# The last product of a feed-forward layer, taken from rounded parts and turned back by two transposes

## What is computed

```python
def _tlin(x, w, s):
    return jnp.einsum('bsi,oi->bso', x, w) * s      # w holds -1, 0 and 1
h = jax.nn.silu(_tlin(x, w1_w, w1_s)) * _tlin(x, w2_w, w2_s)   # 128 -> 512
h = jax.nn.gelu(_tlin(h, h1_w, h1_s), approximate=False)       # 512 -> 512
h = jax.nn.gelu(_tlin(h, h2_w, h2_s), approximate=False)       # 512 -> 512
return _tlin(h, w3_w, w3_s)                                    # 512 -> 128
```

## Time and profile before

| what | value |
|---|---|
| median of 3 runs | 1271.09 us (1270.57 to 1271.78) |
| profiled execution | 1273.35 us, of which the span from first to last instruction is 1271.5 us |
| TensorE clock granted, mean of the span | 0.976 |
| PE busy | 1152.8 us, 91% |
| VectorE busy | 986.7 us, 78% |
| ScalarE busy | 771.9 us, 61% |
| GpSimd busy | 568.4 us, 45% |
| feed-forward layer | about 1071 us to the end, 200 us |

### The profile page before, as it was taken

How to read it: one execution, slowest core, us unless ns; L and a number is a source line. 1 busy time by engine, 2 the same in 40 slices (tenths; PEclk the granted TensorE clock), 3 DMA queues, 4 the chain that set the end, 5 groups by cost and what they waited for, 6 DMA issues and landing times.

```text
span 1271.5 us, 32080 instructions
## 1 busy us (share of the span) xinstructions
PE 1152.8 (91%) x10554; PEld 941.7 (74%) x10554; DVE 986.7 (78%) x2499; ACT 771.9 (61%) x2314; POOL 568.4 (45%) x729
## 2 busy tenths in 40 slices
PE   3888886789898869999999999999999997999997
PEld 3555554688888747777777777777777766999997
DVE  6688885588888777778788778787877876788885
ACT  2445553222222249888989888899888894344342
POOL 2777775444444554444545445445444342011112
PEclk9999998799999989999999999999999998999999
DMA  8000000000000000000000000000000000000000
GB/s 282 10 2 0 0 1 2 1 2 1 0 1 0 1 1 2 1 2 1 2 2 1 0 0 0 0 0 0 0 0 0 2 1 1 6 13 12 8 12 19
DMA packets 14303, 12.32 MB, mean 10 GB/s; under 512 B 1778, under 2 KB 12564, under 8 KB 13972
## 3 DMA queue, kind: packets, MB, share of 16 engines
q1 hardware_dynamic: 14228, 11.34, 2.9%
HBM read 9.24 MB, written 2.10 MB: 9 GB/s over the span
## 4 chain that ended last, share of the span: by engine, by line
PE 56%; DVE 14%; issue 8%; POOL 4%; ACT 1%; DVEq 1%; POOLq 0%; ACTq 0%
PE bank L191 14%; PE bank L976 10%; PE bank L1041 10%; PE bank L1070 10%; PE bank L1083 5%; PE bank L840 4%; POOL rstd L365 2%; DVE stat L298 2%; DVE hT L1230 1%; DVE gg L1222 1%; PE bank L795 1%; DVE yn L314 1%; POOL X L370 1%; DVE mv L303 1%; DVE fh_hi L1191 1%
## 5 line engine op out<-in xcount | busy, mean ns | idle before, releaser
L993 ACT ACTIVATE work<-bank,work 128x256 f32<-128x256 f32 x512 | 236.0, 474 | 60.0 <-DVE work L985 59.2
L985 DVE TENSOR_REDUCE work<-bank 128x2 f32<-128x512 f32 x256 | 164.0, 682 | 113.2 <-PE bank L976 113.2
L1007 POOL TENSOR_TENSOR work<-work 128x512 f32<-128x512 f32 x64 | 66.7, 1041 | 279.0 <-DVE work L1001 279.0
L959 POOL TENSOR_TENSOR work<-work 128x512 f32<-128x512 f32 x128 | 164.3, 1284 | 30.2 <-DVE work L951 15.8
L1013 ACT ACTIVATE work<-work 128x256 f32<-128x256 f32 x384 | 161.7, 509 | 0.0
L1041 PE MATMUL bank<-ident,work 128*128 128x128 f32 x1024 | 141.9, 279 | 5.1 <-DVE work L949 1.6
L1041 PEld LDWEIGHTS bank<-ident,work 128*128 128x128 f32 x1024 | 111.7, 141 | 38.5 <-issue 19.9
L1070 PE MATMUL bank<-work 128*64 128x256 f32 x1024 | 138.5, 392 | 0.5 <-DVE work L1056 0.5
L840 PE MATMUL bank<-WrT,moe_work 128*128 128x128 f32 x1024 | 137.4, 278 | 0.7 <-POOL moe_work L817 0.7
L363 POOL TENSOR_SCALAR ve<-mv 128x2 f32<-128x2 f32 x128 | 28.6, 223 | 240.1 <-DVE mv L303 240.1
L976 PE MATMUL bank<-work 32*128 32x256 f32 x2048 | 130.4, 391 | 2.6 <-ACT work L993 1.6
(11 more groups left out here) (176 smaller groups left out, 2903.9 us busy)
## 6 DMA issues: line engine op xcount, KB each, us to landing
X<-in_x SPq DMA_DIRECT2D x4, 512.0 KB, 5.9
wF<-in_L_ffn_h_w SPq DMA_DIRECT2D x2, 1024.0 KB, 9.7
out<-X SPq DMA_DIRECT2D x16, 128.0 KB, 1.8
w_qkv<-in_L_attn_w_qkv SPq DMA_DIRECT2D x1, 1536.0 KB, 9.2
WrT<-in_L_ffn_Wr SPq DMA_DIRECT2D x1, 1024.0 KB, 5.1
w_out<-in_L_attn_w_out SPq DMA_DIRECT2D x1, 512.0 KB, 10.5
wF<-in_L_ffn_w_w SPq DMA_DIRECT2D x2, 256.0 KB, 8.5
rope_sin<-in_rope_sin SPq DMA_DIRECT2D x1, 256.0 KB, 3.2
```

The lines of the kernel that those rows point to most:

```text
L959: nc.gpsimd.tensor_tensor((QT if kind == "q" else KT)[:, p, a, :], rc[:, ru % 2, :], rs_[:, ru % 2, :], ALU.add).then_inc(c_rope, 1)
L985: nc.vector.tensor_reduce(nmax[:, QUAD * a + j, :], SB_[j][:, :].rearrange("p (t k) -> p t k", t=T), AX.X, ALU.max, negate=True).then_inc( ...
L993: ins = nc.scalar.activation(pr[:, a % 2, j, t, :], SB_[j][:, t * LEN:(t + 1) * LEN], ACT.Exp, bias=nmax[:, h, t:t + 1], accum_out=psum_[: ...
```

## The change

The last product takes parts as the others do. ScalarE rounds `f2` into `f2_hi` (one copy of 128 x 512 behind each half of the gelu), and GpSimd forms `f2_lo = f2 - f2_hi` in two halves at the head of its next step, in front of `rstd` and the residual add. The weight w3 moves into `wF`, so that the test covers it (`wF` grows from 5120 to 5632 columns, `CHECK` from 320 to 352), and gets its parts `w3_hi` (GpSimd, step 0) and `w3_lo` (VectorE, step 0). The product is turned: w3 is stationary, `f2` moves in blocks of 256 tokens, and the result lies by features in `bank7`. ScalarE copies it to `yT`, and two transposes on TensorE bring it back into `Yt`; they stand between the two halves of the second hidden product, which is issued in halves for that. The last sequence keeps the old product behind its last gelu.

```diff
-        wF = sb("wF", [P, (2 + 2 * HID_T) * HID_T * P])
+        wF = sb("wF", [P, (2 + 2 * HID_T) * HID_T * P + HID_T * E])
-        w3T = sb("w3T", [P, HID_T, E])
+        w3T = wF[:, (2 + 2 * HID_T) * HID_T * P:].rearrange("p (k e) -> p k e", k=HID_T)
...
+        ffn_weights.append((w3T, w3S[0][:, :, :], w3S[1][:, :, :]))
+        W3_PIECE = len(ffn_weights) - 1
...
-        def ffn_product(pe, src, wS, written, emptied, base, short):
-            for m in range(2):
+        def ffn_product(pe, src, wS, written, emptied, base, short, halves=range(2)):
+            for m in halves:
...
+        def ffn_round_scalar(act, i, m):
+            b = slice(2 * m, 2 * m + 2)
+            act.wait_ge(d_a2, 2 * i + m + 1)
+            act.wait_ge(d_yt, reached(i))
+            nc.scalar.activation(f2S[0][:, b, :], f2[:, b, :], ACT.Copy).then_inc(d_f2hi, 1)
+
+        def ffn_rest_pool(pool, i):
+            for m in range(2):
+                b = slice(2 * m, 2 * m + 2)
+                wait_apart(pool, d_f2hi, 2 * i + m + 1, s_nhalf, 1)
+                nc.gpsimd.tensor_tensor(f2S[1][:, b, :], f2[:, b, :], f2S[0][:, b, :], ALU.subtract).then_inc(d_f2s, 1)
+
+        def ffn_out_turned_tensor(pe, i, short):
+            if i_is(i, 0):
+                pe.wait_ge(n_xnT[3], SEQS)
+                pe.wait_ge(d_w, EARLY + HID_T + 1)
+            pe.wait_ge(d_f2s, 2 * (i + 1))
+            pe.wait_ge(d_yc, reached(i))
+            for kb in range(HID_T):
+                ins = split_product(VB[:, 0:LEN], (w3S[0][:, kb, :], w3S[1][:, kb, :]),
+                                    (f2S[0][:, kb, :], f2S[1][:, kb, :]), kb == 0, kb == HID_T - 1, short)
+            ins.then_inc(d_yt, 1)
+
+        def ffn_out_scalar(act, i):
+            act.wait_ge(d_yt, i + 1)
+            act.wait_ge(d_y, reached(i))
+            nc.scalar.activation(yT[:, :], VB[:, 0:LEN], ACT.Copy).then_inc(d_yc, 1)
+
+        def ffn_back_tensor(pe, i):
+            pe.wait_ge(d_yc, i + 1)
+            pe.wait_ge(y_ready[FFN], reached(i))
+            for t in range(T):
+                ins = nc.tensor.transpose(Yt[:, t, :], yT[:, t * P:(t + 1) * P], ident[:, :])
+            ins.then_inc(d_y, 1)
...
 # GpSimd, ffn_step(i, p)
-                if not (i_is(i, 0)):
+                if i_is(i, 0):
+                    pool.wait_ge(c_v, 2 * QUADS * SEQS)
+                    ffn_weights_pool(pool, (W3_PIECE,))
+                else:
+                    ffn_rest_pool(pool, i - 1)
                     norm_pool(pool, 4, i - 1, 0)
...
 # VectorE, ffn_step(i, p), behind ffn_in_vector(dve, i + 1)
+                if i_is(i, 0):
+                    ffn_weights_vector(dve, (W3_PIECE,))
...
 # ScalarE, ffn_step(i, p)
-                act.wait_ge(d_y, reached(i))
-                gelu(i, 1, f2, d_m2, d_a2)
+                if not i_is(i, 0):
+                    ffn_out_scalar(act, i - 1)
+                    act.wait_ge(d_f2s, 2 * i)
+                for m in range(2):
+                    gelu(i, 1, f2, d_m2, d_a2, (m,))
+                    if not i_is(i, SEQS - 1):
+                        ffn_round_scalar(act, i, m)
...
 # TensorE, ffn_step(i, p)
-                        ffn_out_tensor(pe, i - 1)
+                        ffn_out_turned_tensor(pe, i - 1, short)
...
-                    ffn_product(pe, f1S, h2S, d_m2, d_a1, 2 * i, short)
+                    ffn_product(pe, f1S, h2S, d_m2, d_a1, 2 * i, short, (0,))
+                    if not i_is(i, 0):
+                        ffn_back_tensor(pe, i - 1)
+                    ffn_product(pe, f1S, h2S, d_m2, d_a1, 2 * i, short, (1,))
```

More of the change, by code:

```diff
@@ L172, in block_kernel @@
         yf = third("yf", PR + 4 * HALF_FF, 2, T, E)
+        w3S = [third(f"w3_{part}", PR + 4 * HALF_FF + 2 * T * E + n * HID_T * E, HID_T, E, dt=F32R)
+               for n, part in enumerate(("hi", "lo"))]
         tg = third("tg", OTS, 2, 2, LEN)
         gg = third("gg", OTS + 4 * LEN, 2, 2, LEN)
+        f2S = [third(f"f2_{part}", OTS + 8 * LEN + n * HALF_FF, HID_T, LEN, dt=F32R) for n, part in enumerate(("hi", "lo"))]
         hS = [third(f"fh_{part}", V_ + n * HALF_FF, HID_T, LEN, dt=F32R) for n, part in enumerate(("hi", "lo"))]
@@ L183, in block_kernel @@
         xS = [third(f"fx_{part}", H1_ + 2 * HID_T * HID_T * P + n * LEN, LEN, dt=F32R) for n, part in enumerate(("hi", "lo"))]
+        yT = third("yT", H1_ + 2 * HID_T * HID_T * P + 2 * LEN, LEN)
         third_set.close()
@@ L1248, in ffn_product @@
                 ins.then_inc(written, 1)
+        d_f2hi, d_f2s, d_yt, d_yc = (sem(n) for n in ("d_f2hi", "d_f2s", "d_yt", "d_yc"))
+        def ffn_round_scalar(act, i, m):
[28 more added lines that the diff above has]
+            ins.then_inc(d_y, 1)
         def ffn_out_tensor(pe, i):
@@ L1252, in ffn_out_tensor @@
             pe.wait_ge(y_ready[FFN], reached(i))
-            if i_is(i, 0):
-                pe.wait_ge(n_xnT[3], SEQS)
             for t in range(T):
@@ L1299, in _ @@
                              (h2T, w["L1_ffn_h2_w"].rearrange("(k p) o -> p k o", p=P)),
-                             (w3T[:, :, :], w["L1_ffn_w3_w"].rearrange("(k p) o -> p k o", p=P)),
+                             (w3T, w["L1_ffn_w3_w"].rearrange("(k p) o -> p k o", p=P)),
                              (fs[:, :, :], w["L1_ffn_scales"]),
@@ L1706, in _, with gelu @@
                 sa_out_scalar(act, SEQS - 1, t, VB[:, t * E:(t + 1) * E])
-            def gelu(i, product, dst, written, done):
-                for m in range(2):
+            def gelu(i, product, dst, written, done, halves=range(2)):
+                for m in halves:
                     act.wait_ge(written, 2 * i + m + 1)
```

## The result

The changed kernel takes 1303.3 us (median of 4 runs, 1301.15 to 1303.71), the kernel before 1271.43 us (4 runs, 1270.57 to 1272.84). The ratio is 1.0246, 95% interval [1.0228, 1.0264]: slower by 31.9 us. 1301 was forecast, and the range 1291 to 1307 holds the time. The profiled execution took 1303.37 us with a span of 1301.6, against 1273.35 and 1271.5.

The account below looks back on a forecast made before the run. VectorE's loop with its rstd wait was taken as the bound, not TensorE. Subtractions 28.4, transposes 0.35, w3_hi 0.45 and test 0.8 sum to 30.0 us, giving 1301 us from 1271.09; range 1291 to 1307 (8 in 10).

Parts of the forecast that it names:

- What bounds: Feed-forward period of 11.8 us: VectorE's loop with its rstd wait bounds; TensorE follows with about 0.25 us to spare.
- Rivals 3 and 4: Feed-forward period: subtractions meet VectorE at no cost, 1271 to 1272 us (0.04); or TensorE decides, 1265 us (0.03).
- rival 3: Subtractions fall while VectorE works from PSUM or waits for rstd, costing nothing: 1271 to 1272 us; chance 0.04.
- The subtractions: Behind the residual add, GpSimd and VectorE take turns; each pair costs 2.03 us, 14 pairs 28.4 us.
- rival 1: GpSimd goes from residual add through both subtractions without letting VectorE in: 14 x 2.4 us, 1306 us; chance 0.09.
- rival 2: Only one of two subtractions is paid, the second partly under gg: 14 x 1.1 us, 1288 us; chance 0.06.
- Is another engine late next?: Lengthened feed-forward period: TensorE would wait 1.1 us for fh_lo but stay behind VectorE.
- The end: Last step: transposes come on the path inside the second hidden product, +0.35 us, besides the last subtraction pairs.
- 0.35 for transposes: Last step: transposes stand inside the second hidden product, on the path, +0.35 us.
- The head: Early steps: w3_hi holds up xn, +0.45 us; the larger test holds up VectorE, +0.8 us; w3_lo costs nothing.
- The test's 0.8 us: GpSimd's longer test instructions: one of three per sequence holds up VectorE by some 0.05 us, +0.8 (0 to 3.2).
- Sum: All terms together: 28.4 + 0.35 + 0.45 + 0.8 = 30.0 us added to the median 1271.09 us.

Follow-up runs that it names:

- e1: Changed kernel with GpSimd's two subtractions cut to one column from sequence 1 on; products keep their shapes: 1273.29 us, ratio 1.0000 to the kernel before.
- e3: Kernel before plus ScalarE's rounding copies and GpSimd's subtractions, results unused, old last product kept: 1301.53 us, ratio 1.0226.
- e5: e3 with each subtraction made to wait until VectorE turns to work from PSUM: 1273.66 us, ratio 1.0000 to the kernel before.
- e2: Changed kernel with only the second of the two subtractions cut to one column from sequence 1 on: 1290.0 us, ratio 1.0146 to the kernel before.
- e10: Changed kernel with only sequence 14's two subtractions, in the last step, cut to one column: 1301.69 us, ratio 1.0215 to the kernel before.
- e8: Changed kernel with subtractions placed by VectorE's PSUM time, turned product between the second hidden product's halves, transposes behind them: 1278.93 us, ratio 1.0049 to before.
- e4: Kernel before with only w3 moved into the tested weights, test columns 320 to 352: 1272.94 us, ratio 1.0000.
- e6: Kernel before with VectorE's yn moved behind the rounding of a later step, to cover its rstd wait: 1270.71 us, ratio 0.9987.
- e8b: e8 run again unchanged, for a second trace of its end: 1279.04 us, ratio 1.0050 to the kernel before.
- e9: e8 combined with the yn edit of e6: 1274.75 us, ratio 1.0012 to the kernel before.

## Why the prediction was right

**What bounds.** VectorE's loop with `rstd`, not TensorE's 98%: shown from both sides. e1 takes 0.41 us a step from TensorE and the time stands still, with 0.4 us more waiting a period; e3 leaves TensorE as it was, adds GpSimd work, and the time goes up as with the whole change. Rivals 3 and 4 fall with the changed kernel itself, and e5 shows that the condition of rival 3 can be made true.

**The subtractions.** 14 x 2.03 = 28.4 was forecast. Twelve periods measure 2.06 each. Taking turns was the mechanism: `fx_lo` goes first (rival 1 would have it last), and e2 shows 1.11 for the first subtraction alone (rival 2 would have two cost that much). The Trainium skill, page "SBUF — State Buffer", section "SBUF: two separate sides", has the lock held for the whole instruction; an estimate by that, 2 x 1.27, has the pair cost 2.54 us, and the runs show 2.06. The blocking is as it says. The price is less, because the one that has waited is over sooner than its own length: in the period shown, the first subtraction ends at 1172.10 and the long `ff_hi` 0.28 us behind it, not 0.42; the second ends at 1173.53, 1.15 us behind `ff_hi` and not 1.27, and the long `ff_lo` 0.54 behind that, not 0.69.

**Is another engine late next?** No, as forecast. TensorE waits for `fh_lo` 1.14 us a period (forecast 1.1). That wait costs nothing in the period.

**The end** was mis-sized: 4.4 us forecast (two blocks, 0.35 for transposes), 5.5 measured. The step that missed it took the matmuls behind the wait at the 0.12 us of the earlier trace rows; they came at 0.21, at half clock, for 3.4 us. Sixteen of them make 1.4 us, and with the two blocks that is all of the 5.5. The 0.35 for the transposes doesn't show: e1, which has them without the subtractions, takes 28.6 us from its last `fx_lo` to the end, no more than before's 28.77, and e10 leaves no room for them either. In e10's trace, without the last two subtractions, both the wait and the half clock are gone; that the wait doesn't always bring it is what e8 shows. e3, which has no transposes in its end, has the half clock too, and 33.5 us.

**The head.** 1.25 us were forecast for `w3_hi` and the test; the traces show `fx_lo` of step 2 at 1100.52 before and 1100.42 after. Two single executions can't give this term, and the one of before was unusual. Its clock read half for 6.4 us around the first products of the layer, and the one of after was back sooner (busy times and clock, before first; each in its own execution):

```profile
1053.00:1059.40 6.40, 6.07 (x28) 6.10 (x29) 1.92 (x7) 1.67 (x5) 0.95 (x2) 0.50 0.00 0
```

```profile
1057.50:1059.40 1.90, 1.90 (x19) 1.87 (x17) 0.00 (x0) 0.20 (x1) 0.00 (x0) 1.00 0.00 0
```

24 matmuls there took 5.46 us before and 4.42 after. They started 0.98 us later in the changed kernel (1054.31 against 1053.33), and its `fx_lo` of step 0 came 0.48 sooner (1074.24 against 1074.72): some 1.5 us of loss were hidden. That this is chance, and not the change, the other traces show: from 1050 to 1070 us the mean clock is 0.83 in before's and 0.91 in each of the eleven others, e4, e5 and e6 among them. From step 0 to step 2 the changed kernel then takes 26.18 us against 25.80, 0.4 more; e5 and e4, which have no `w3_hi`, have 25.81 and 25.88, e2, e8 and e8b 26.12 to 26.22, but e1 and e10 27.06 and e3 26.83, for which I have no cause. The block of `xn` by `w3_hi` can be seen directly, 0.87 us against the 0.60 of the earlier trace rows, so 0.27 where 0.45 was forecast:

```profile
1079.18 0.87 DVE L347 TENSOR_SCALAR xn<-X,mv,rstd 128x128 f32<-128x128 f32 x2 [1.22 <-POOL rstd L369]
```

The test's 0.8 us stay unproved (e4).

**Sum.** 24.7 for twelve periods, 5.5 for the end and -0.1 at the head make 30.1, the difference of the spans (1301.6 and 1271.5); forecast 30.0. The mechanism and its price were right: 28.4 us were forecast for fourteen pairs, and fourteen times 2.06 are 28.8. That the whole sum meets the spans to 0.1 us is luck: the end came out 1.1 us above its forecast, the head 1.35 below it, mostly by the clock of one execution. The medians differ by 31.9, because the profiled execution of before was 2 us above the median of its 4 runs and that of after was at its. The forecast's median, taken by adding the sum to 1271.09, is short by that. Against the 1273.5 of the larger set of before (29 runs) the changed kernel's 1303.3 is 29.8 more, but it wasn't run again beside them.

## What to carry to other kernels

An instruction added on GpSimd is priced by what VectorE does at that moment: beside rounding copies and two-input subtractions from SBUF to SBUF it costs VectorE nearly its own length, beside `gg` and `hT`, which read PSUM, nothing, beside the statistics nothing either, and a wait on the right semaphore moves it from the one to the other (28 us to 0 here). Read which engine's wait ends last in a period before counting busy shares: TensorE at 98% was given 3% less work and nothing came of it. And look at the last step by itself, where work that was hidden in the loop comes on the path and an idle TensorE may come back at half its clock.

## What the runs showed of the hardware that I had not expected

- **Two of 1.27 us cost 2.06, one costs 1.11.** In the changed kernel GpSimd and VectorE take turns instruction by instruction, and each that waited is over 0.12 to 0.15 us sooner than its length says. GpSimd's subtractions read 1.42 to 1.70 us there and 1.27 in e5, since they too wait.
- **Half clock behind one wait.** In the last step of the changed kernel TensorE had been at full clock throughout the repeating stretch, waited 2.81 us, and the clock then read half for 3.4 us. e2 (behind a wait of 1.8 us), e3, e8b and e9 (2.1 us each) show the same at their ends; e8's profiled execution had e8b's wait of 2.12 us to the hundredth and no half clock. Before, e1, e5, e6 and e10, in which TensorE waits at most 1.1 us at a time in the last step up to the last gelu, show none there. What decides between e8 and e8b these runs don't show.
- **A freed wait brings little.** VectorE's waits for `rstd` fell from 14.6 us to 4.3 in twelve periods (e6), which gave 0.2 us a period: TensorE, 98% busy before, is 99.5% busy then, and the loop of `fh`, products, `gg` and `hT` is as long.
- **Statistics pass beside a subtraction.** VectorE's `stat<-yf` keeps its 0.49 us while GpSimd subtracts (e8), though both work in SBUF.
